# The last level of a blocked triangular inverse in both column halves of TensorE, with half of the evictions on VectorE and the second product behind the output projection

## The reference, cut to what matters

```python
def step(state, inp):
    q_t, k_t, v_t, g_t, b_t = inp
    state = state * jnp.exp(g_t)[:, :, None, None]
    kv_mem = jnp.einsum('bhd,bhde->bhe', k_t, state)
    delta = (v_t - kv_mem) * b_t[:, :, None]
    state = state + jnp.einsum('bhd,bhe->bhde', k_t, delta)
    out_t = jnp.einsum('bhd,bhde->bhe', q_t, state)
    return (state, out_t)
```

## Time and profile before

| | |
|---|---|
| median of 3 runs | 4379.56 us (4370.98 to 4380.68) |
| the profiled execution | 4372.25 us |
| its span, first to last instruction | 4370.5 us |
| mean granted TensorE clock | 0.985 of full speed |
| busy in the span: PE, DVE, ACT, POOL | 96%, 77%, 52%, 10% |

### The profile page before, as it was taken

How to read it: one execution, slowest core, us unless ns; L and a number is a source line. 1 busy time by engine, 2 the same in 40 slices (tenths; PEclk the granted TensorE clock), 3 DMA queues, 4 the chain that set the end, 5 groups by cost and what they waited for, 6 DMA issues and landing times. The chain is left out here.

```text
span 4370.5 us, 82252 instructions
## 1 busy us (share of the span) xinstructions
PE 4191.9 (96%) x30773; PEld 2602.9 (60%) x30773; DVE 3359.7 (77%) x8547; ACT 2278.0 (52%) x5209; POOL 448.6 (10%) x406
## 2 busy tenths in 40 slices
PE   7899999999999999999999999998699999999898
PEld 4566666666666666666666666666344444444443
DVE  5888887888888888878888778875446989898950
ACT  3555555555555555555555555554245545554542
POOL 0111111111111111111111111110000000000000
PEclk9999999999999999999999999999899999999999
DMA  2111111111110112111111101100203445444520
GB/s 74 41 37 38 33 40 33 37 33 35 42 33 30 37 38 66 45 33 33 35 38 40 35 30 37 38 28 6 91 1 121 147 137 162 147 157 140 174 80 10
DMA packets 202415, 263.46 MB, mean 60 GB/s; under 512 B 18174, under 2 KB 101378, under 8 KB 202018
## 3 DMA queue, kind: packets, MB, share of 16 engines
q1 hardware_dynamic: 202018, 258.20, 18.5%
HBM read 249.24 MB, written 8.91 MB: 59 GB/s over the span
## 5 line engine op out<-in xcount | busy, mean ns | idle before, releaser
L470 PE MATMUL bank<-xnT,w_qkv 128*128 128x512 f32 x2048 | 926.4, 595 | 4.9 <-ACT raw L744 4.2
L470 PEld LDWEIGHTS bank<-xnT,w_qkv 128*128 128x128 f32 x2048 | 373.6, 191 | 402.0 <-issue 383.3
L1053 DVE SCALAR_TENSOR_TENSOR conv<-raw,conv_w,conv 128x1024 f32<-128x1024 f32 x384 | 516.1, 1344 | 121.5 <-ACT conv L721 112.3
L583 PE MATMUL bank<-w_out_unit,oT 128*128 128x512 f32 x1024 | 505.7, 617 | 7.9 <-ACT oT L790 7.9
L544 PE MATMUL bank<-w_z_unit,xnT 128*128 128x256 f32 x2048 | 487.1, 381 | 0.0
L544 PEld LDWEIGHTS bank<-w_z_unit,xnT 128*128 128x128 f32 x2048 | 371.1, 191 | 40.4 <-issue 0.2
L744 ACT COPY raw<-bank 128x512 f32<-128x512 f32 x256 | 149.5, 584 | 351.2 <-PE bank L470 348.1
L1277 PE MATMUL bank<-xnT_f,w_gu 128*128 128x512 f32 x704 | 326.8, 608 | 5.0 <-ACT xnT_f L1734 4.0
L1295 PE MATMUL bank<-w_down,hidden 128*128 128x512 f32 x704 | 318.6, 596 | 1.9 <-DVE x_blocks L1337 1.9
L1285 PE MATMUL bank<-xnT_f,w_gu 128*128 128x512 f32 x704 | 317.7, 594 | 0.0
L838 ACT ACTIVATE squares<-o 128x128 f32<-128x128 f32 x512 | 153.9, 302 | 297.7 <-DVE o L1097 261.5
(11 more groups left out here) (234 smaller groups left out, 7811.3 us busy)
## 6 DMA issues: line engine op xcount, KB each, us to landing
rows_b<-bc_rows SPq DMA_DIRECT2D x256, 256.0 KB, 3.4
rows_c<-bc_rows SPq DMA_DIRECT2D x256, 256.0 KB, 3.5
w_qkv<-in_w_qkv SPq DMA_DIRECT2D x128, 256.0 KB, 2.9
decay<-gc_rows SPq DMA_DIRECT2D x64, 512.0 KB, 3.9
w_z_unit<-in_w_z SPq DMA_DIRECT2D x32, 512.0 KB, 4.5
w_out_unit<-in_w_out SPq DMA_DIRECT2D x32, 512.0 KB, 5.0
x_after<-x SPq DMA_DIRECT2D x16, 256.0 KB, 2.0
x_blocks<-x_after SPq DMA_DIRECT2D x4, 1024.0 KB, 12.1
```

The lines of the kernel that those rows point to most:

```text
L470: made = e.matmul(PROJ[:, :], w_qkv[:, p % 2, j, :], xnT[:, n // HK, j, h * BANK:(h + 1) * BANK], start=j == 0, stop=j == KT - 1)
L583: made = e.matmul(OB[:, :], oT[:, r, :], w_out[:, N % 2, r, :], start=r == 0, stop=r == REP - 1)
L1053: e.scalar_tensor_tensor(acc, raw[:, i % 2, tap:tap + T], conv_w[:, tap, col:col + 1], acc, ALU.mult, ALU.add).then_inc(on["conv"], 1)
```

## The change

Level 2 alone is changed, for both halves of every unit.

- In part 0 the even matrices still go into PSUM partitions 64 to 127, the odd ones now into partitions 0 to 63. In part 1 it is the other way round. The output's partitions are PE's columns, so the matrices of a group alternate between the two halves of the columns. The rows (partitions 0 to 63 in part 0, 64 to 127 in part 1) are those of before.
- ACT evicts the even matrices alone (two instructions of half the size). DVE gets two new instructions in each of the two slots: the negation of the odd ones from PSUM partitions 0 to 63 into `off`, partitions 64 to 127, ahead of the state, and the copy of the odd ones from PSUM partitions 64 to 127 into `invT`, partitions 0 to 63, in the last loop of the slot.
- Part 1 of level 2 goes from ahead of the output projection to behind it. Parts 1 of levels 0 and 1 stay.
- Part 1 waits for DVE's negation too, the scan and the next inverse for DVE's copy; `INV_STEPS` counts the two new steps.

```diff
--- before.py
+++ after.py
@@ -124,7 +124,7 @@
 
 LINKS = NC - 1
 BASE_STEPS = 4 + 4 + 3 * (BASE - 2) + 1
-INV_STEPS = 9
+INV_STEPS = 11
 K, Q, V0, V1 = range(4)
 
 
@@ -230,6 +230,10 @@
             return decay[:, N % 2, :, HALF * a:HALF * (a + 1), :]
 
         norm_rows = lambda N: conv[:, (4 * N + K) % 3, 0:BANK]
+
+
+        lower_at = lambda i: (slice(hp, P), slice(0, hp))[i % 2]
+        upper_at = lambda i: (slice(0, hp), slice(hp, P))[i % 2]
         evens = inv[:, :, :].rearrange("p n (s h w) -> p n s h w", s=2, h=2)[:, :, :, 0, :]
         tile_ps = inv_ps[:, :, 0:32]
         evens_ps = tile_ps.rearrange("p n (s w) -> p n s w", s=2)
@@ -370,12 +374,14 @@
                     e.wait_ge(on["mask"], H + 1)
                     if H > 0:
                         e.wait_ge(on["invT"], H)
+                        e.wait_ge(on["inv_dve"], INV_STEPS * H)
                 elif level < 2:
                     e.wait_ge(on["inv_dve"], INV_STEPS * H + ((0, 2), (3, 6))[level][part])
                 elif part == 0:
                     e.wait_ge(on["inv_dve"], INV_STEPS * H + 9)
                 else:
                     e.wait_ge(on["inv_neg"], H + 1)
+                    e.wait_ge(on["inv_dve"], INV_STEPS * H + 10)
                 for i in range(NC):
                     if level == 0:
                         for b in range(4):
@@ -400,16 +406,16 @@
                             made = e.matmul(tile_ps[low, i, :], ttT[low, i, low], off[low, i, 0:32],
                                             start=True, stop=True)
                     elif part == 0:
-                        made = e.matmul(inv_ps[hp:P, i, :], lt[0:hp, i, hp:P], inv[0:hp, i, :],
+                        made = e.matmul(inv_ps[lower_at(i), i, :], lt[0:hp, i, hp:P], inv[0:hp, i, :],
                                         start=True, stop=True)
                     else:
-                        made = e.matmul(inv_ps[0:hp, i, :], off[hp:P, i, :], ttT[hp:P, i, hp:P],
+                        made = e.matmul(inv_ps[upper_at(i), i, :], off[hp:P, i, :], ttT[hp:P, i, hp:P],
                                         start=True, stop=True)
                 made.then_inc(on["inv_pe"], 1)
 
-            def inverse_step(slot, part):
+            def inverse_step(slot, part, levels):
                 for a in range(2):
-                    for level in range(3):
+                    for level in levels:
                         n = unit_at_only(slot, INVERSE + 4 * a + level)
                         if n is not None:
                             inverse(n, a, level, part)
@@ -507,6 +513,7 @@
                         e.wait_ge(on["inv_zero"], 1)
                     if t % HALF == 0:
                         e.wait_ge(on["invT"], 2 * N + t // HALF + 1)
+                        e.wait_ge(on["inv_dve"], INV_STEPS * (2 * N + t // HALF + 1))
                     if at > 0:
                         e.wait_ge(on["o_add"], at)
                     for r in range(REP):
@@ -547,7 +554,7 @@
                     if i == 1:
                         made.then_inc(on["z_pe"], 1)
 
-                inverse_step(slot, 0)
+                inverse_step(slot, 0, (0, 1, 2))
 
                 for a in range(2):
                     n = unit_at_only(slot, 9 + 4 * a)
@@ -572,7 +579,7 @@
                                         start=True, stop=True)
                     made.then_inc(on["a_pe"], 1)
 
-                inverse_step(slot, 1)
+                inverse_step(slot, 1, (0, 1))
 
                 if n_out is not None:
                     N, t = n_out, t_out
@@ -583,6 +590,8 @@
                         made = e.matmul(OB[:, :], oT[:, r, :], w_out[:, N % 2, r, :],
                                         start=r == 0, stop=r == REP - 1)
                     made.then_inc(on["wout_pe"], 1)
+
+                inverse_step(slot, 1, (2,))
 
                 n = unit_at_only(slot, 6)
                 if n is not None:
@@ -782,7 +791,7 @@
                     if n is not None:
                         H = 2 * n + a
                         e.wait_ge(on["inv_pe"], 6 * H + 5)
-                        e.mul(off[hp:P, :, :], inv_ps[hp:P, :, :], -1.0).then_inc(on["inv_neg"], 1)
+                        e.mul(off[hp:P, 0::2, :], inv_ps[hp:P, 0::2, :], -1.0).then_inc(on["inv_neg"], 1)
 
                 n, t = unit_at(slot, WOUT)
                 if n is not None:
@@ -824,7 +833,7 @@
                     if n is not None:
                         N = n
                         e.wait_ge(on["inv_pe"], 6 * (2 * N + a) + 6)
-                        e.copy(invT_i(a)[0:hp, :, hp:P], inv_ps[0:hp, :, :]).then_inc(on["invT"], 1)
+                        e.copy(invT_i(a)[0:hp, 0::2, hp:P], inv_ps[0:hp, 0::2, :]).then_inc(on["invT"], 1)
 
                 if n_scan is not None:
                     N, t = n_scan, t_scan
@@ -1071,6 +1080,12 @@
                     n = unit_at_only(slot, 9 + 4 * a)
                     if n is not None:
                         evict_pair(n, a, 1)
+                for a in range(2):
+                    n = unit_at_only(slot, INVERSE + 4 * a + 2)
+                    if n is not None:
+                        e.wait_ge(on["inv_pe"], 6 * (2 * n + a) + 5)
+                        e.tensor_scalar(off[hp:P, 1::2, :], inv_ps[0:hp, 1::2, :], -1.0, None, ALU.mult).then_inc(
+                            on["inv_dve"], 1)
                 if n_scan is not None:
                     N, t = n_scan, t_scan
                     at = 8 * N + t
@@ -1115,6 +1130,10 @@
                                 for q in (0, 64):
                                     e.tensor_copy(invT_i(a)[q:q + 32, :, q + 32:q + 64], tile_ps[q:q + 32, :, :]).then_inc(
                                         on["inv_dve"], 1)
+                    n = unit_at_only(slot, INVERSE + 4 * a + 2)
+                    if n is not None:
+                        e.wait_ge(on["inv_pe"], 6 * (2 * n + a) + 6)
+                        e.tensor_copy(invT_i(a)[0:hp, 1::2, hp:P], inv_ps[hp:P, 1::2, :]).then_inc(on["inv_dve"], 1)
                     n = unit_at_only(slot, 10 + 4 * a)
                     if n is not None:
                         base_inverse(n, a, 0)
```

## The result

| | before | with the change |
|---|---|---|
| median | 4375.27 us (4 runs, 4368.48 to 4380.68) | 4411.43 us (4 runs, 4409.70 to 4414.75) |
| the profiled execution, its span | 4372.25, 4370.5 us | 4414.75, 4413.0 us |
| a period of 8 slots in the steady part | 92.66 us | 93.74 us |

The ratio of the runs is 1.0077, with a 95% interval of 1.0057 to 1.0096: the changed kernel is slower by 25 to 42 us. Forecast were 4399 (range 4355 to 4425) and slower by 19; the medians differ by 36. A fourth run of the kernel before, 4368.48, took its median from the 4379.56 of the forecast to 4375.27.

The account below looks back on a forecast made before the run. PE, busy 96%, was taken as the bound, weighed against a DVE chain with 0.89 us to spare. 29 x 1.63 lost, less 30 x 0.83 and 3 gained, gave +19 us: 4399 us, range 4355 to 4425 (own range 4383 to 4412).

Parts of the forecast that it names:

- The column halves: PE in level 2: matrices alternating between column halves run side by side, making each group 0.46 us shorter.
- Rival 3: Level 2 on PE: the pairs do not run side by side, giving 4457 us; chance 0.06.
- The A slot: Slot where DVE's copy precedes base section 2: DVE's chain starts 2.47 us later, making PE 1.63 us late.
- the wait for `oT`: Output projection after part 0: PE, ready at 1.16, starts line 583 at 1.65, a new wait of 0.49 us.
- The B slot: Slot where DVE's copy follows base section 2: enough slack remains, so PE gains 0.83 us.
- The sum: Whole kernel: losses of 47.3 us less gains of 24.9 and 3 give +19 us, 4399 us.
- the edge term: Few slots at both ends, without a projection or with DVE idle: together gain about 3 us.
- What would show it: Trace signs: parts at 0.68 us, DVE idle 2.7 before its copy, new PE waits, period about 93.45.
- rival 1: DVE's copy, first of the two slots: DVE absorbs the late start and PE's gain shows, 4339 us; chance 0.14.

## Why the prediction was right, point by point

The mechanism and the sign were right. The size was not: 19 us were forecast, the medians differ by 36 and the two spans by 42.5. That 4411.43 still lies under the 4412 of the forecast's own range is in part luck, since the forecast stood on a median of 4379.56 that a fourth run lowered by 4.3.

- **The column halves.** Forecast 0.46 us for a group, from a third tile in level 1 that cost nothing. Measured 1.14 - 0.68 = 0.46. The Trainium skill's rule that weight loads overlap only across row groups ("TensorE: Matmul & The Clock Gate", Part 3, The mechanism) would by itself have left 1.14; the trace disagrees for these tiles, which share their rows, and the measurement decides. Rival 3 is out.
- **The A slot.** Forecast: projection at 1.65, part 1 at 3.56, the next group at 4.17, section 2 at 4.64. Measured: 1.66, 3.57, 4.18, 4.66. The chain was to be late by 2.47 and PE by 1.63; it was late by 2.49 and PE by 1.72 (20.25 against 18.53). Another 0.1 follows in the next slot, since line 521's first record takes longer after a wait. The runs with the copy behind and with part 1 back show that this chain is the main cause; the wait for `oT`, which the prediction has too, is worth 0.78 us of a period.
- **The B slot.** Forecast a gain of 0.83, measured 0.75 (12.82 to 12.07 us from one start of line 514 or 521 to the next). The slack left behind the residual was 1.86, above the "more than 1" of the text.
- **The sum.** The period was forecast to grow by 0.80 and grew by 1.08: 0.19 too little in the A slot, 0.08 too much gain in the B slot. Over 27 steady periods of the trace this is 29.3 us, not 21.6.
- **What failed is the edge term.** "The few at both ends, without a projection or with DVE idle, gain about 3 together." In the two traces the time to the first chunk of the third unit grew by 3.2 us, the last three units' scans by 11.8, the rest of the program shrank by 1.9. With the 29.3 that is the 42.5 by which the two spans differ. At the end the sign was wrong for two reasons. The slots there lack the qkv projection. I took that as slack for DVE, when it is PE that has 3.4 us less to do (line 470 before) between the output projection and the work that waits for DVE. Behind the last B slot but one the reader of the residual waits 2.47 us instead of 0.57 (lines 521 at 2996.13, 514 before at 2958.98), and in the last A slot PE waits at the addition to `x`:

```profile
3035.90 0.33 PE L461 MATMUL bank<-ident,kq 128*128 128x128 f32 x1
3036.70 0.68 PE L521 MATMUL bank<-v_tok,invT 128*128 128x128 f32 x4 [0.47 <-DVE invT L1136]
3040.34 0.44 PE L539 MATMUL bank<-ident,o 128*128 128x128 f32 x2 [2.96 <-DVE x L927]
3040.62 2.99 PE L551 MATMUL bank<-w_z_unit,xnT 128*128 128x256 f32 x8
```

  In the kernel before, line 532 waited 0.64 at this place. The second reason is a term that the sum didn't have, the granted clock. These are the stretches of the last three units' scans, first with the change, then before:

```profile
2856.16:3097.15 240.99, 212.79 (x2051) 150.96 (x2049) 169.36 (x504) 111.81 (x321) 29.26 (x26) 0.95 0.06 19
2823.64:3052.81 229.17, 208.62 (x2052) 150.75 (x2050) 161.94 (x490) 114.03 (x321) 28.58 (x26) 0.98 0.06 20
```

  A mean of 0.95 over 241 us is about 24 us at the lower level, 1.2 GHz, and 0.98 over 229 about 9 (estimates from these two rows). In three slots of the last two units DVE keeps PE waiting no longer than before, and yet they last 1.68, 1.67 and 1.63 us more. The first begins behind the 2.47 us of waiting named above, and its z projection lasts 3.57 us instead of 1.89. The kernel before has one such slot there, with a z projection of 2.82:

```profile
2996.91 3.57 PE L551 MATMUL bank<-w_z_unit,xnT 128*128 128x256 f32 x8
```

  At the start the very first part 1 waits for DVE's negation, which there stands behind 7.1 us of base inverse work (140.90 to 148.03):

```profile
148.63 1.12 PE L412 MATMUL bank<-invT,off 64*64 64x64 f32 x16 [4.50 <-DVE off L1087]
```

- **What would show it.** Forecast and seen: both parts at 0.68, DVE idle ahead of its copy in the A slot (2.52, forecast 2.7) and not in the B slot, waits for residual and state, a period of more than 92.66. The wait for `oT` shows as 0.34 in the bracket; counted from when PE was ready (1.16) it is 0.50, as forecast.
- **The rivals.** DVE did have 17 us idle a period, and 75.24 of 92.66 us busy did not protect it (rival 1). Once the copy stood behind the section, the slack of 0.89 us was enough (0.34 of it was left) and PE's gain showed.

## What to carry to other kernels

Before work is handed to an engine with idle time, look at what is queued behind the wait that comes with it, and at the slack at the end of that queue: a copy of 0.4 us cost over 2 us here because it waited ahead of 15 us of chained work with 0.9 to spare, and 0.17 us in the slot where 1.9 were to spare. When a group is moved behind another one, ask what it had been covering; here it was the eviction that the other one needs, so that eviction has to go first on its engine. With the same column halves on PE and the same instructions on every engine, the time was 0.8% above or 1.2% below the kernel before, by two orders alone, that of the copy on DVE and that of `oT` on ACT.

## What the runs showed of the hardware that was not expected

- Evictions by DVE from PSUM in one half of the partitions into SBUF in the other take 0.42 to 0.43 us for 64 x 256 float32. Its eviction of 128 x 256 that stays on its partitions takes 0.42. On ACT, in the run with all evictions there, a negation of 64 x 256 takes 0.38 within a half and from one half to the other, a copy 0.37.
- With four matrices of one column half ahead of four of the other, 16 records take 0.96 us, against 1.14 in one half and 0.68 alternating. The first record of the second four starts 0.29 us after the first of all, where the first four alone would keep PE for about 0.46. So PE starts on the second half before the first is through, but not from the start.
- In the last A slot PE stood nearly idle for 3.6 us, and behind that the granted clock is 0.63 of full speed on the mean, that is partly at the lower of its two levels, 1.2 GHz. The z projection took 2.99 us there instead of 1.89. So a late DVE was paid for twice in this slot. Not every such wait is followed by the lower level: line 521 at 3029.13 had waited 2.94 us, and the granted clock behind it stayed at 1.00.

```profile
3036.70:3040.30 3.60, 0.68 (x4) 0.49 (x4) 3.19 (x15) 1.09 (x5) 0.22 (x1) 1.00 0.01 2
3040.30:3044.90 4.60, 4.55 (x18) 4.03 (x19) 0.40 (x1) 1.47 (x4) 0.00 (x0) 0.63 0.00 0
```
